# Mixture of experts by sorted blocks: a counting sort and indirect DMAs in place of all sixteen experts for every token

## The reference

```
logits = xn @ wg + bg                                # 16 experts
vals, idx = top_k(logits, 4)                         # ties: the lower index first
gates = softmax(vals);  gate_full = scatter of gates to 16 columns, 0 elsewhere
h = einsum('th,ehd->etd', xn, w1) + b1               # 128 -> 256, columns interleaved a, b
a = min(h[..., ::2], 7);  b = clip(h[..., 1::2], -7, 7)
s = a * sigmoid(1.702 * a) * (b + 1)
y = einsum('eti,eih->eth', s, w2) + b2
out = x + einsum('eth,te->th', y, gate_full)
```

## Time and profile before

| | |
|---|---|
| time, median of 3 runs | 1819.68 us |
| the profiled execution's own time (its span) | 1818.1 us |
| TensorE busy | 1450.2 us, 80% |
| VectorE busy | 1475.4 us, 81% |
| ScalarE busy | 1025.9 us, 56% |
| GpSimd busy | 20.0 us, 1% |
| DMA | 65.76 MB, mean 36 GB/s |

### The profile page before, as it was taken

The page is one execution under the profiler, slowest core; times in us unless marked ns, Lnnn a source line. Parts: engine busy times, 40 slices in busy tenths (PEclk is TensorE's granted clock), DMA queues, the critical chain, the costliest instruction groups (busy, mean ns, idle before and its releaser), DMA issues. The chain is left out here.

```text
span 1818.1 us, 38591 instructions
## 1 busy us (share of the span) xinstructions
PE 1450.2 (80%) x13559; PEld 1057.3 (58%) x13559; DVE 1475.4 (81%) x3537; ACT 1025.9 (56%) x1764; POOL 20.0 (1%) x41
## 2 busy tenths in 40 slices
PE   1569989999999999999977878724666567677776
PEld 0546666666666666666655666513555555466665
DVE  6785139888888888888877999859888887599996
ACT  0564348777777777777766777601111111577774
POOL 3000000000000000000000000000000000000000
PEclk9779999999999999999998899965556655788887
DMA  7000000000000000000001222250332210111111
GB/s 210 0 0 1 1 0 1 1 1 1 0 0 0 0 0 0 0 0 0 1 1 41 87 103 99 87 151 6 91 86 62 62 50 16 49 54 53 53 49 33
DMA packets 80860, 65.76 MB, mean 36 GB/s; under 512 B 3680, under 2 KB 65504, under 8 KB 80736
## 3 DMA queue, kind: packets, MB, share of 16 engines
q1 hardware_dynamic: 70128, 58.26, 10.3%
q10 hardware_dynamic: 10608, 5.79, 1.1%
HBM read 34.68 MB, written 29.36 MB: 35 GB/s over the span
## 5 line engine op out<-in xcount | busy, mean ns | idle before, releaser
L911 ACT ACTIVATE glu_a<-moe_a,b1s 128x512 f32<-128x512 f32 x256 | 176.7, 690 | 130.6 <-PE moe_a L822 128.3
L916 ACT ACTIVATE b_raw<-moe_b,b1s 128x512 f32<-128x512 f32 x256 | 176.3, 689 | 0.7 <-PE moe_b L822 0.5
L968 DVE TENSOR_TENSOR glu_a<-glu_a,moe_g 128x512 f32<-128x512 f32 x256 | 175.8, 687 | 0.0
L975 DVE TENSOR_TENSOR h_lo<-glu_a,h_hi 128x512 fp32r<-128x512 f32 x256 | 175.3, 685 | 0.6 <-ACT h_hi L927 0.6
L960 DVE SCALAR_TENSOR_TENSOR glu_a<-glu_a,b_raw 128x512 f32<-128x512 f32 x256 | 175.3, 685 | 0.1
L927 ACT ACTIVATE h_hi<-glu_a 128x512 fp32r<-128x512 f32 x256 | 161.8, 632 | 18.6 <-DVE glu_a L968 3.2
L951 DVE TENSOR_SCALAR b_raw<-b_raw 128x512 f32<-128x512 f32 x256 | 108.9, 425 | 72.9 <-ACT b_raw L916 72.9
L820 PE MATMUL moe_a<-x_hi,w_hi 128*128 128x512 f32 x256 | 127.2, 497 | 2.8 <-DVE w_lo L987 2.8
L849 PE MATMUL moe_y<-h_hi,w_hi 128*128 128x512 f32 x256 | 102.0, 399 | 2.7 <-DVE h_lo L975 2.7
L820 PE MATMUL moe_b<-x_hi,w_hi 128*128 128x512 f32 x256 | 101.7, 397 | 0.0
L821 PE MATMUL moe_a<-x_lo,w_hi 128*128 128x512 f32 x256 | 101.2, 395 | 0.0
(11 more groups left out here) (269 smaller groups left out, 3304.5 us busy)
## 6 DMA issues: line engine op xcount, KB each, us to landing
kq_scratch<-kq_out SPq DMA_DIRECT2D x16, 512.0 KB, 3.2
kq_in<-kq_scratch SPq DMA_DIRECT2D x16, 512.0 KB, 5.0
acc<-in_L_attn_inputs SPq DMA_DIRECT2D x8, 512.0 KB, 10.1
xq_scratch<-qT SPq DMA_DIRECT2D x16, 256.0 KB, 2.0
v_scratch<-v_out SPq DMA_DIRECT2D x16, 256.0 KB, 2.0
k_scratch<-k_out SPq DMA_DIRECT2D x16, 256.0 KB, 2.3
k_in<-k_scratch SPq DMA_DIRECT2D x8, 512.0 KB, 7.7
v_in<-v_scratch SPq DMA_DIRECT2D x8, 512.0 KB, 7.5
```

What stands on the lines that cost most here:

```text
L911: act.activation(glu_a[e % 4][:, :], ps_a[u][:, :], ACT.Gelu_apprx_sigmoid, bias=w["b1"][:, 0, e:e + 1]).then_inc(a_glu, 1)
L916: act.activation(b_raw[u][:, :], ps_b[u][:, :], ACT.Identity, bias=w["b1"][:, 1, e:e + 1])\
L968: dve.tensor_tensor(a, a, ps_g[u][:, :], ALU.mult).then_inc(weighted, 1)
L975: dve.tensor_tensor(h_lo[e % 2][:, :], glu_a[e % 4][:, :], h_hi[e % 2][:, :], ALU.subtract)\
```

## The change

Each token's rows go only to its four experts. The tokens are treated in two halves of 32 groups of 128 (HALVES = 2, HSUB = 32). For each half:

1. VectorE numbers the chosen experts of each token, and finds with two small products (strictly upper triangle of ones, and ones) and prefix scans how many earlier tokens chose the same expert. Each expert's rows start at a multiple of 512, so each (token, k) has a slot in a DRAM buffer `xs[h]` of BLOCKS = 48 blocks of 512 rows (32 for 16384 pairs, and 16 for rounding up).
2. GpSimd scatters the rows `xm` to the slots: one indirect DMA for each k and group of 128 tokens, 128 rows of 512 B, 128 DMAs a half.
3. A loop over 96 blocks, both halves in one: SP loads the block's rows and, by a value that it reads from SBUF, the weights of its expert from tables in DRAM; TensorE transposes the rows (`turn_x`), ScalarE and VectorE split them in two parts, six up products, activation, cut and multiply as before, and one float32 product down (`down_proj`) without the split and without the gate; VectorE adds b2 (`take_y`) and SP stores the rows in `ys[h]`.
4. GpSimd gathers each token's four result rows by the same slots, 128 indirect DMAs a half, and VectorE adds them to `acc` with their gates as per-partition scalars (`combine`), then takes the statistics (`count`). The first half's are placed in the loop over the second half's blocks, seven of its eight tiles; the others follow the loop.

The setup pass now clears the slot rows in DRAM with 12 stores of 2 MB from a tile of zeros, and stores the expert tables (upper and lower part of w1: 4.2 MB; w2, b2 and b1: 2.1 MB); both are on SP's queue behind its loads. The turn pass keeps `xm` in SBUF for all tokens and no longer makes `xmT` and `xsT`; the scaling and its transpose move into the token stage, which is now the first part of `routed_pass`, with its gates gone. The diff, cut to its core:

```diff
+HALVES = 2
+HSUB = NSUB // HALVES
+HTILES = TILES // HALVES
+BLOCKS = HSUB * P * TOPK // TILE + EXPERTS
+ALL_BLOCKS = HALVES * BLOCKS
+SLOTS = BLOCKS * TILE
+ROUND_MAGIC = 1.5 * 2.0 ** 23
+WROW = 2 * DIM + 2 * DIM
+VROW = DIM + DIM + 2
...
+                sp.wait_ge(rows_zeroed, 1)
+                for rows in f["xs"]:
+                    for n in range(0, BLOCKS, 8):
+                        sp.dma_start(rows.rearrange("(n p j) d -> p n (j d)", p=P, j=SUBS)[:, n:n + 8, :],
+                                     f["no_rows"][:, :].unsqueeze(1).to_broadcast([P, 8, SUBS * DIM]))\
+                          .then_inc(f["slots_zeroed"], 16)
+                sp.wait_ge(tables_ready, 1)
+                sp.dma_start(f["w_up"].rearrange("e p k -> p e k"), f["up_table"][:, :, :].bitcast(F32))\
+                  .then_inc(f["tables_stored"], 16)
+                sp.wait_ge(tables_ready, 2)
+                sp.dma_start(f["w_down"].rearrange("e p k -> p e k"), f["down_table"][:, :, :])\
+                  .then_inc(f["tables_stored"], 16)
...
+                sp.wait_ge(f["tables_stored"], 32)
...
+        XB, YG, AHEAD = 4, 8, 2
...
+                pool.wait_ge(f["slots_zeroed"], 16 * (ALL_BLOCKS // 8))
+                for h in range(HALVES):
+                    for k in range(TOPK):
+                        pool.wait_ge(slots_ready, TOPK * h + k + 1)
+                        for j in range(HSUB):
+                            pool.indirect_dma_start(
+                                f["xs"][h], bass.IndirectOffsetOnAxis(ap=slot[:, h, k, j:j + 1], axis=0),
+                                xm[:, HSUB * h + j, :], None).then_inc(scattered[h], 16)
+                for h in range(HALVES):
+                    for i in range(XB):
+                        pool.wait_ge(y_stored[i], 16 * (BLOCKS // XB) * (h + 1))
+                    for j in range(HSUB):
+                        n = HSUB * h + j
+                        if n >= YG:
+                            pool.wait_ge(combined, TOPK * SUBS * ((n - YG) // SUBS) + SUBS * (TOPK - 1) + n % SUBS + 1)
+                        for k in range(TOPK):
+                            pool.indirect_dma_start(
+                                yg[n % YG][:, k, :], None, f["ys"][h],
+                                bass.IndirectOffsetOnAxis(ap=slot[:, h, k, j:j + 1], axis=0))\
+                                .then_inc(gathered[n % YG], 16)
...
+                def load_x(b):
+                    h = b // BLOCKS
+                    if b % BLOCKS == 0:
+                        sp.wait_ge(scattered[h], 16 * TOPK * HSUB)
+                    if b >= XB:
+                        sp.wait_ge(x_turned, b - XB + 1)
+                    sp.dma_start(xb[b % XB][:, :, :],
+                                 f["xs"][h][rows_of(b), :].rearrange("(p j) d -> p j d", j=SUBS))\
+                      .then_inc(x_loaded[b % XB], 16)
+
+                def load_w(b):
+                    h = b // BLOCKS
+                    if b % BLOCKS == 0:
+                        sp.wait_ge(experts_ready, h + 1)
+                    at = b % BLOCKS
+                    e = sp.value_load(expert_of[0:1, h, at:at + 1], min_val=0, max_val=E - 1)
+                    sp.dma_start(up_w[b % XB][:, :, :, :].rearrange("p a s d -> p (a s d)").bitcast(F32),
+                                 f["w_up"][bass.ds(e, 1), :, :].rearrange("a p k -> p (a k)"))\
+                      .then_inc(w_loaded[b % XB], 16)
+                    sp.dma_start(down_w[b % XB][:, :],
+                                 f["w_down"][bass.ds(e, 1), :, :].rearrange("a p k -> p (a k)"))\
+                      .then_inc(w_loaded[b % XB], 16)
+
+                def store(b):
+                    sp.wait_ge(y_ready, b + 1)
+                    sp.dma_start(f["ys"][b // BLOCKS][rows_of(b), :].rearrange("(p j) d -> p j d", j=SUBS),
+                                 yb[b % XB][:, :, :]).then_inc(y_stored[b % XB], 16)
+
+                for s in range(-AHEAD, ALL_BLOCKS + XB):
+                    if s >= XB:
+                        store(s - XB)
+                    if 0 <= s < ALL_BLOCKS:
+                        load_w(s)
+                    if s + AHEAD < ALL_BLOCKS:
+                        load_x(s + AHEAD)
+                for i in range(XB):
+                    sp.wait_ge(y_stored[i], 16 * (ALL_BLOCKS // XB))
...
+                rank(0)
+                rank(1)
+                pe.wait_ge(rank_taken, 4)
+                sweep(pe, TILES, [(0, turn_s), (1, score), (2, mix)])
+
+                def turn_x(b, u):
+                    pe.wait_ge(x_loaded[u], 16 * (b // XB + 1))
+                    wait_free(pe, x_lo_ready, b, 1)
+                    for j in range(SUBS):
+                        mm = pe.transpose(ps_x[u % 2][:, P * j:P * j + P], xb[u][:, j, :], w["ident"][:, :])
+                    mm.then_inc(x_turned, 1)
+
+                def up(b, u):
+                    hi, lo = x_hi[u % 2][:, :], x_lo[u % 2][:, :]
+                    pe.wait_ge(x_lo_ready, b + 1)
+                    pe.wait_ge(w_loaded[u], 32 * (b // XB + 1))
+
+                    def product(place, s):
+                        pe.matmul(place[:, :], up_w[u][:, 0, s, :], hi, start=True, stop=False)
+                        pe.matmul(place[:, :], up_w[u][:, 0, s, :], lo, start=False, stop=False)
+                        return pe.matmul(place[:, :], up_w[u][:, 1, s, :], hi, start=False, stop=True)
+
+                    wait_free(pe, glued, b, 1)
+                    product(ps_a[u % 2], 0).then_inc(up_a, 1)
+                    wait_free(pe, lined, b, 1)
+                    product(ps_b[u % 2], 1).then_inc(up_b, 1)
+
+                def down_proj(b, u):
+                    pe.wait_ge(multiplied, b + 1)
+                    wait_free(pe, y_ready, b, 1)
+                    for j in range(SUBS):
+                        mm = pe.matmul(ps_y[u % 2][:, P * j:P * j + P], glu[u % 2][:, P * j:P * j + P],
+                                       down_w[u][:, 0:DIM], start=True, stop=True)
+                    mm.then_inc(down, 1)
+
+                pe.wait_ge(gelued, PC * TILES)
+                pe.wait_ge(added, TILES)
+                sweep(pe, ALL_BLOCKS, [(0, turn_x), (2, down_proj), (1, up)], turns=XB)
...
+                def split_x(b, u):
+                    act.wait_ge(x_turned, b + 1)
+                    wait_free(act, up_b, b, 1)
+                    act.activation(x_hi[u % 2][:, :], ps_x[u % 2][:, :], ACT.Copy).then_inc(x_hi_ready, 1)
+
+                def squash(b, u):
+                    bias = down_w[u]
+                    act.wait_ge(up_a, b + 1)
+                    wait_free(act, down, b, 1)
+                    act.activation(glu[u % 2][:, :], ps_a[u % 2][:, :], ACT.Gelu_apprx_sigmoid,
+                                   bias=bias[:, 2 * DIM:2 * DIM + 1]).then_inc(glued, 1)
+                    act.wait_ge(up_b, b + 1)
+                    wait_free(act, multiplied, b, 1)
+                    act.activation(lin[u % 2][:, :], ps_b[u % 2][:, :], ACT.Identity,
+                                   bias=bias[:, 2 * DIM + 1:2 * DIM + 2]).then_inc(lined, 1)
+
+                sweep(act, ALL_BLOCKS, [(0, split_x), (1, squash)], turns=XB)
...
+                choose(0)
+                find_slots(0)
+                choose(1)
+                find_slots(1)
+                to_share(0)
+                add(0)
+                find_experts(0)
+                find_gates(0)
+                add(1)
+                to_share(1)
+                add(2)
+                find_experts(1)
+                find_gates(1)
+                for t in range(3, TILES):
+                    add(t)
+                dve.wait_ge(added, TILES)
...
+                def lower_x(b):
+                    u = b % 2
+                    dve.wait_ge(x_hi_ready, b + 1)
+                    if b >= 2:
+                        dve.wait_ge(up_b, b - 1)
+                    dve.tensor_tensor(x_lo[u][:, :], ps_x[u][:, :], x_hi[u][:, :], ALU.subtract).then_inc(x_lo_ready, 1)
+
+                def multiply(b):
+                    u = b % 2
+                    dve.wait_ge(lined, b + 1)
+                    dve.tensor_scalar(lin[u][:, :], lin[u][:, :], 1.0 + LIMIT, 1.0 - LIMIT, ALU.min, ALU.max)\
+                       .then_inc(cut, 1)
+                    dve.wait_ge(glued, b + 1)
+                    dve.wait_ge(cut, b + 1)
+                    dve.scalar_tensor_tensor(glu[u][:, :], glu[u][:, :], GLU_LIMIT, lin[u][:, :], ALU.min, ALU.mult)\
                        .then_inc(multiplied, 1)
...
+                def take_y(b):
+                    dve.wait_ge(down, b + 1)
+                    if b >= XB:
+                        dve.wait_ge(y_stored[b % XB], 16 * (b // XB))
+                    dve.tensor_tensor(yb[b % XB][:, :, :], sub_view(ps_y[b % 2]),
+                                      down_w[b % XB][:, DIM:2 * DIM].unsqueeze(1).to_broadcast([P, SUBS, DIM]),
```

(38 more changed lines are left out.)

715 lines of the change are left out of this document (282 added, 433 removed).

## The result

The changed kernel takes 2280.64 us (median of 4 runs, 2276.85 to 2282.78), the kernel before beside it 1820.12 us (4 runs): a ratio of 1.2526, 95% interval 1.2506 to 1.2545. It is 460 us slower; the prediction had it 83 us slower, with a range that ended at 2080. The profiled execution has a span of 2279.9 us.

The account below looks back on a forecast made before the run. Experts' 256 steps, with TensorE and VectorE nearly full, bound the kernel; setup 108, turn 66, tokens 172, experts 521, tail 165 and later passes 869 sum to 1901 us of span, so 1903, range 1760 to 2080.

Parts of the forecast that it names:

- Setup: Setup pass: 25 MB of zeros on SP's queue make it end near 108 us instead of 48.8, +59.
- Turn pass: Turn pass: without `xs`, its root, transposes and copies it takes 66 us against 85, -19.
- c: POOL's time for one indirect DMA, estimated at 1.2 us between a floor of 0.33 and a ceiling of 2.0.
- The tail: Behind the last block: second half's 128 gathers and last combine, 165 us; half 1's scatters and half 0's gathers hidden earlier.
- Routing and tokens: Before the first block: the longer of 162 us of tokens and 167 of first-half scatters, plus 5, makes 172 us.
- Clock and pitch of blocks: Expert blocks: 4.55 us each at full clock, 7.0 at half, 5.08 at 0.85; 96 blocks make 488 us.
- rival (c): Expert blocks: TensorE's clock at half throughout, +182 us, 2085 in all; chance 0.07.
- Second half's blocks: Blocks beside first-half gathers: 5.08 us each, plus 25 us for `combine` and `count`, gathers hidden while c < 1.9.
- Loads of weights and rows: DMA in each block: 0.9 MB at 180 GB/s, costed at nothing, with a floor of 3.5 us.
- Rivals: Three alternatives to the forecast: cheap indirect DMAs (1786 or 1735 us, 0.28), dear ones (2107, 0.15), half clock (2085, 0.07).
- (b): Scatters and gathers: each indirect DMA costs a 2.0 us round trip, 102 us before and 102 behind blocks, 2107; chance 0.15.
- TensorE's bubble: Expert blocks: TensorE idles 1.4 us while down products wait for a 2.03 us chain through ACT and VectorE.

Follow-up runs that it names:

- spaced_zeros: Changed kernel with a 128x512 memset behind each scatter and each first-half gather, and the stores of zeros moved from setup to the turn pass: 1958.7 us.
- few_scatters: Changed kernel with 8 of the 256 scatters left, the same work per block: 1988.1 us.
- drained: Changed kernel with 128x256 memsets behind most scatters and first-half gathers, zeros in the turn pass, up products split around down products, halves run out separately: 1816.95 us, ratio 0.9988.
- scatters_gap256: Changed kernel with a 128x256 memset on GpSimd, and a wait for it, behind each scatter: 2041 us.

## Why the prediction was wrong, step by step

- **Setup** (108, by the zeros that hold SyncE's queue): 107.5, at 344 GB/s and a DMA share of 1.01. Right. `spaced_zeros`, with the zeros beside the turn pass, has its first scatter at 150.8 instead of 193.7 us, so 43 of the 59 us could be had back.
- **Turn pass** (66): 65.5. Right.
- **c** (1.2 us for an indirect DMA, between 0.33 and 2.0): 1.27 in scatters, 1.26 in gathers. Right, and so is what follows for exposed ones: 128 gathers in the tail. The tail was 180 instead of 165, of which 128 x 0.06 = 8 are `c`; the other 7 are not accounted for.
- **Routing and tokens** (5 + max(162, 13 + 128 c) = 172): 472. This is the step that failed. The `max` puts POOL's 167 us beside TensorE's 162 and takes the larger, as if the two had nothing in common but the slots. Measured, the 256 scatters (193.7 to 528 us) and the tiles nearly exclude one another, so the terms add, and the second half's scatters, which the tail paragraph hid "in the 488 us", were paid here as well: 256 x 1.27 = 325 us of scatters in which little else ran. Without them, `few_scatters` has its first block at 350.7, 5 over the forecast's 346 and 10 over the 341 of its sum with nothing to wait for but the tiles.
- **Clock and pitch of blocks** (0.85, 5.08 us): the first 48 blocks had 1.00 and 227.1/48 = 4.73 us, 4.60 in steady state, near the warm end of 4.55. The clock was read off rows of other stages with a like busy share (0.81 and 0.88 at 72 to 74%); here TensorE was busy 65% and had 1.00, so the term was 17 us too dear (48 x 5.08 = 244). The worry of rival (c) did not come up where GpSimd was quiet; in the second half the granted clock was 0.78, and there TensorE had those pauses.
- **Second half's blocks** (244 + 25 for joins = 269 beside gathers costed at nothing): 357.6. The same failed step: 128 gathers were taken as hidden while c < 1.9. The waits of that stage have TensorE waiting for `glu` up to 30 us at a time, each time beside a burst of gathers, and it goes on a few us after the burst. `few_scatters`, with its gathers as they were, takes as long (last down products at 936.7); in `spaced_zeros`, with a pause behind each gather of the first half, the 96 blocks take 508 us from first to last down product instead of 580.
- **Loads of weights and rows** (costed at nothing): right. 196 GB/s, and no down or up product waits for a load in the steady state, nor at 3.36 us a block, at 303 GB/s in `drained` from 350 to 510 us.
- **Rivals**: none of the three was this. (b), dear DMAs, has the right sign and 2107, but its mechanism, a round trip of 2.0 us each, is refuted by 1.27. The Trainium skill, page "SBUF — State Buffer", section "Who interferes with whom", says that a DMA never contends with a compute engine and that TensorE and ScalarE never wait on anyone. For plain DMAs the trace agrees (159 products in 40 us beside them, as without); for indirect ones it does not (15), and here the measurement decides. I had read nothing that spoke of this and had no rival for "POOL's work slows the others": the trace of before had 20 us of GpSimd in all, none of it an indirect DMA, and what it can't show needs a bound also on its neighbours, not only on its own price.

The sign was right, but most of the loss came from what the prediction had at nothing. Its own reason is there as well, and smaller: with the scatters spaced the change stands at 2041 (`scatters_gap256`), 12% over the kernel before, and with the gathers spaced too and the zeros moved at 1959 (`spaced_zeros`), 8% over. How that rest divides among the pauses, the joins, the tail and TensorE's bubble wasn't taken apart.

## What to carry to other kernels

For a kind of instruction that the trace has never shown, bound both its own time and what the other engines get done beside it; a few of them put into the kernel before, where nobody needs them, show both. Count indirect DMAs (here 512 at 1.27 us, 650 us of GpSimd), and leave a pause with a wait behind each (here the memset of 128x256) or put them where nothing else runs. Where a loop waits for a chain through two other engines, cut the first engine's work so that part of it lies between the chain's links (4.60 to 3.36 us a block here), and stop when one engine's row sets the end.

## What the runs showed of the hardware that I had not expected

- Indirect DMAs from GpSimd, 1.27 us apart, take the other engines of the core down to a tenth: 44 products of TensorE in 120 us instead of 474, 22 operations of VectorE instead of 200, 14 of ScalarE instead of 143. Beside 256 of them the kernel before loses 305 us.
- It doesn't depend on rows or bytes (64 rows: 43 products), nor on the software queue or the number of packets (plain DMAs from GpSimd each 0.54 us, 32 packets each as well: 159 products in 40 us, as without).
- It fades between 1.27 and 1.58 us from one to the next, where GpSimd waits for a memset behind each (96, 259, 300 products in 50 us at 1.36, 1.47 and 1.58, against 18 at 1.27 with nothing between); uneven pauses of the same mean without that wait do little (34).
- What in the indirect form does it, and through what the engines are starved, stays open: the runs show late instructions on TensorE, VectorE and ScalarE, in the experts' long loop and in a short one, in the short one with no packet on the queues of code, and not the path.
